# A change in who rounds tokens and who multiplies mean by rstd in a fused attention and FFN block

## The chip, the cores and the metric

The kernel runs on one core of one Trainium2 chip. The metric is the device time of one execution in microseconds; the median of several runs counts. The engines are PE (TensorE), DVE (VectorE), ACT (ScalarE), POOL (GpSimd) and SP (SyncE). Each works through its own queue in order, and they meet at semaphores.

## What is computed

One transformer block over 2048 tokens of width 128, modulated by a conditioning vector c:

```python
mod = silu(c) @ wmod              # sa, ca, ga, sb, cb, gb
h = layernorm(x) * (1 + ca) + sa
x = x + ga * (softmax(causal((h@Wq+bq) @ (h@Wk+bk).T / sqrt(128))) @ (h@Wv+bv) @ Wo + bo)
h = layernorm(x) * (1 + cb) + sb
mask = top-4 of 16 blocks of softmax(h @ w_router + b_router)
x = x + gb * (sum over blocks of mask * relu(h @ w1_block + b1_block) @ w2_block + b2)
```

All is float32. Where precision counts, the kernel splits an operand into a rounded part (hi, type fp32r) and a rest (lo), and multiplies in three passes: hi by hi, lo by hi, hi by lo.

## The kernel before

The 2048 tokens are 16 tiles of 128 and four groups of 512 (`NG = 4`, `GT = 4` tiles each). Norms 0 to 3 are the first layernorm of the four groups, norms 4 to 7 the second. The projections of queries and keys are folded into one matrix (`fold_hi`, `fold_lo`), and the value and output matrices into `back`. So the attention weights multiply the normalized tokens themselves, in the halves `z_hi` and `z_lo`.

The order of work is written out by hand: one plan per engine, a list of words such as `j0` or `e12`, a letter for the kind of step and a number for its group, tile or part (lines 43 to 68). `run` calls the steps in that order, so each engine's queue is its plan. SP has no plan: it loads the inputs in order and then stores the results as they are made (lines 402 to 409).

The steps that matter here:

- ACT (`SCALAR_PLAN`): `j0` and `j1` copy the two halves of group 0's transposed tokens to `zt_hi` (line 598). `z3` makes `fold_hi` (544), `z6` copies w1, `z11` makes `lift2` (557, 558), `q` rounds the queries to `g_hi` (606), `n` the transposed norms (602), `a` applies a norm to a group as x times rstd plus a bias (591), `e` are the exponentials of one score tile, twice, to `p_hi` and `p_full` (620, 627), or once to `p_last` (618), `c` copies the context (633), `h` rounds the hidden layer (656), `y` the output.
- DVE (`VECTOR_PLAN`): `g` makes the statistics of a norm (687, 690), `z3` `fold_lo` (880), `u` `zt_lo` of group 0 (721), `z10` copies the modulation (893, 894), `v` applies norm 1 (714), `s` are the row maxima of score chunks (744, 749, 755, 759), `n` and `q` the rests (728, 733), `b` puts the maxima into a row of `g_lo` (767, 769), `i` hides later keys (778), `m` and `c` are the router's logits and the choice (832), `f` the results (863).
- POOL (`GPSIMD_PLAN`): `p` is the power (variance + eps) to -0.5 of a norm; with it go, for norms that ACT applies (2 to 7), a negated mean (428) and its product with rstd (433), which is ACT's bias. `u` are the token halves of a group: a rounding copy to `z_hi` (444) and the rest `z_lo` (445). `l` makes `p_lo` (513), `k` `hid_lo` (519).
- PE (`TENSOR_PLAN`): `n` transposes a norm, `q` projects, `a` is a score chunk for the maxima (989), `s` the scores in three passes (1028, 1029, 1041), `w` the weighted sum (929, 930, 933), `o` the output projection (1073), `m` transposes the choice (1110), `h` and `d` the two layers of the FFN.

Results go through `res`, two buffers of 512 columns for four groups. The results of groups 2 and 3 therefore wait on DVE for the stores of groups 0 and 1 (lines 860 and 900).

Of the kernel before, what the change touches and what calls it, by code (L numbers as in the profile page):

```python
# [22 lines left out]
P = 128  # L23
GT = 4
# [16 lines left out]
FIRST_MAXES = ("a0", "a1", "a2", "a3")  # L41

TENSOR_PLAN = """
i1 i0 i3 z0 i2 z10 z1 n0 z2 z6 z3 q0 z4 z7 a0 a1 a2 a3 n1 p2 p1 p0 b0 q1 s0 s1 a4 a5 z5 s2 a6 s3 a7 n2 w0 a8 a9
w1 w2 w3 a10 a11 p4 z9 p6 z8 b1 q2 o0 n3 s4 a12 p5 a13 s5 s6 a14 s7 a15 a16 w4 s8 a17 w5 a18 s9 a19 q3 a20 s10
a21 w6 a22 s11 a23 w7 a24 w8 b2 w9 a25 w10 s12 a26 s13 a27 s14 w11 s15 a28 a29 w12 s16 o1 s17 s18 s19 a30 a31
s20 w13 s21 a32 w14 a33 s22 a34 w15 a35 s23 w16 a36 a37 w17 w18 a38 a39 n4 w19 w20 b3 w21 r0 w22 s24 s25 h0 z11
s26 w23 s27 s28 m0 s29 w24 n5 o2 s30 s31 h1 s32 r1 w25 w26 w27 h2 s33 w28 s34 w29 m1 w30 h3 n6 s35 s36 s37 r2
s38 w31 w32 w33 h4 w34 w35 w36 s39 m2 w37 w38 w39 h5 d0 o3 d1 d2 d3 h6 h7 d4 h8 d5 h9 d6 n7 d7 h10 r3 d8 h11 d9
d10 m3 y0 h12 v12 h13 v13 y1 d11 h14 v14 h15 v15 d12 d13 y2 d14 d15 t0 y3 t1  # L50
"""
SCALAR_PLAN = """
z0 z1 j0 j1 z3 z6 z11 q0 z4 n1 z9 a2 q1 e0 z5 e1 e2 n2 e3 c0 z13 z12 a3 z8 q2 e4 n3 e5 e6 e7 e8 q3 e9 e10 e11
e12 e13 c1 e14 e15 e16 z7 e17 e18 e19 e20 a4 e21 n4 e22 e23 a5 e24 e25 e26 c2 m0 e27 e28 e29 n5 e30 h0 e31 e32
a6 h1 e33 m1 e34 n6 e35 e36 e37 z14 h2 h3 e38 e39 c3 h4 m2 h5 y0 h6 h7 a7 h8 n7 h9 y1 h10 m3 h11 h12 h13 y2 h14
h15 y3 z15
"""
VECTOR_PLAN = """
j0 z0 j1 a0 z1 a1 g1 z3 u0 u1 z10 g2 v1 s0 s1 s2 s3 q0 n1 b0 g3 s4 s5 z5 s6 s7 q1 s8 s9 s10 s11 n2 b1 x0 s12 s13
s14 q2 s15 s16 n3 s17 i8 s18 s19 i9 s20 s21 i10 s22 s23 s24 i11 b2 s25 z6 s26 s27 q3 s28 s29 g4 x1 g5 s30 i20  # L60
s31 s32 s33 s34 s35 i21 s36 s37 i22 s38 s39 n4 i23 b3 m0 c0 h0 x2 n5 g6 h1 m1 c1 n6 i36 h2 h3 i37 m2 i38 c2 i39
h4 h5 x3 g7 h6 h7 h8 h9 n7 h10 m3 c3 h11 f0 k12 k13 f1 k14 k15 f2 f3 t0 t1
"""
GPSIMD_PLAN = """
z0 z1 z4 j0 j1 u0 p1 z7 p2 z6 z8 l0 l1 l2 p3 u1 z11 u2 l4 l5 l6 l7 l8 l9 z10 l10 l12 l13 l14 l15 l16 l17 l18 p4
l19 l20 l21 p5 l22 z9 u3 l24 l25 l26 l27 l28 l29 l30 p6 l31 k0 l32 l33 k1 l34 l35 l36 k2 l37 l38 k3 k4 k5 p7 k6
k7 k8 k9 k10 k11 z12
"""


def adaln_attention_sparse_ffn(nc, x_in, wq_in, bq_in, wk_in, bk_in, wv_in, bv_in, wo_in, bo_in,
# [61 lines left out]
    with ExitStack() as ctx:  # L133
# [22 lines left out]
        hid_full = sb("hid_full", [P, 2, GW])  # L156
        hid_hi, hid_lo = sb("hid_hi", [P, NH, GW], F32R), sb("hid_lo", [P, NH, GW], F32R)
        y_sb = sb("y_sb", [P, 2, GW])
        res = sb("res", [P, 2, GW])
        future, unseen = sb("future", [P, GW]), sb("unseen", [P, P])  # L160

        wq, wk, wv, wo = (sb(n, [P, P]) for n in ("wq", "wk", "wv", "wo"))
# [84 lines left out]
        xn_by_act, xn_by_dve = sem("xn_by_act"), sem("xn_by_dve")  # L247
        nmax_s, score_hid = sem("nmax_s"), sem("score_hid")
        dve_step, pool_step = sem("dve_step"), sem("pool_step")
        xt_mm, nt_hi_s, nt_lo_s, z_tok_s = sem("xt_mm"), sem("nt_hi_s"), sem("nt_lo_s"), sem("z_tok_s")  # L250
        q_mm, q_hi_s, q_lo_s = sem("q_mm"), sem("q_hi_s"), sem("q_lo_s")

        turn_mm, turn_out, first_max_mm, first_max = (sem(n) for n in ("turn_mm", "turn_out", "first_max_mm", "first_max"))
# [105 lines left out]
        def store_row(queue, i):  # L359
            t = GT // 2 + i  # L360
            queue.wait_ge(row_res_s, i + 1)
            queue.dma_start(out_tiles[NG - 1][:, t:t + 1, :],
                            res[:, (NG - 1) % 2, t * P:(t + 1) * P].rearrange("p (i d) -> p i d", d=D)).then_inc(stored[NG - 1], 16)

        block = ctx.enter_context(nc.Block())

        @block.sync
        def _(sp):
            def load(dst, src, done):
                sp.dma_start(dst, src).then_inc(done, 16)  # L370
# [24 lines left out]
            load_bias(BO, bo_in, bias_vo_in_s)
            load_column(B2, b2_in, b2_in_s)
            load_x(3)
            load(b1_row[:], row(b1_in), b1_in_s)
            load(wr[:], wr_in, wr_in_s)
            load(br_row[:], row(br_in), wr_in_s)  # L400

            for n in range(NG):
                g, part = n, result_part(n)
                sp.wait_ge(res_s, n + 1)
                sp.dma_start(out_tiles[g][:, part.start // P:part.stop // P, :],
                             res[:, g % 2, part].rearrange("p (i d) -> p i d", d=D)).then_inc(stored[g], 16)
            store_row(sp, 1)
            for g in range(NG):
                sp.wait_ge(stored[g], 16 if g < NG - 1 else 48)

        @block.gpsimd
        def _(pool):
# [10 lines left out]
            def power(n):  # L423
                k, g = n // NG, n % NG
                t = slice(g * GT, g * GT + GT)
                pool.wait_ge(stats, n + 1)
                if scalar_applies(n):
                    ahead(pool.tensor_scalar(neg_mean[:, k, t], mv[:, k, t, 0], -1.0, None, ALU.mult))
                step(pool.tensor_scalar(rstd[:, k, t], mv[:, k, t, 1], EPS, None, ALU.add))
                last = pool.tensor_tensor(rstd[:, k, t], rstd[:, k, t], pow_half[:], ALU.pow)  # L430
                if scalar_applies(n):
                    step(last)
                    last = pool.tensor_tensor(mean_rstd[:, k, t], neg_mean[:, k, t], rstd[:, k, t], ALU.mult)  # L433
                last.then_inc(power_s, 1)
# [90 lines left out]
        def _(act):  # L525
# [132 lines left out]
            def y_copy(n):  # L658
# [616 lines left out]
```

## Time and profile before

| what | value |
|---|---|
| median of three runs | 113.96 us (113.64 to 114.23) |
| the profiled execution, its time | 113.55 us |
| its span, first to last instruction | 111.8 us |
| granted TensorE clock over the span | 1.0 of full |
| PE busy 15.5 to 21.7 us | 6.16 of 6.20 us |
| DVE, ACT, POOL busy in it | 5.65, 4.34, 4.85 us |
| PE busy 21.7 to 25.5 us | 3.67 of 3.80 us |
| DVE, ACT, POOL busy in it | 3.66, 3.80, 3.50 us |

The profile is of one execution. Times of rows are counted from the span's start; a row of a timeline has the start, the duration, the engine, the line of the kernel, the operation, what is written and read, the shape and the count, and in brackets the idle time of the engine ahead of it with what ended it. Neighbours on one engine overlap a little: a start to start distance is what an instruction costs its queue. PEld is PE's weight load, which runs ahead of the matmul of its line.

### The profile page before, as it was taken

The page shows a single profiled execution, that of the slowest core. Times are in us where ns is not written, and L with a number is a line of the kernel's source. Part 1 is how long each engine was busy: PE and PEld are TensorE (multiplying, and loading weights), DVE is VectorE, ACT ScalarE, POOL GpSimd, SP SyncE. Part 2 cuts the span into 40 slices and gives each one's busy share as a digit, 9 for nine tenths or more (in the row PEclk, how much of TensorE's full clock was granted, in tenths as well). Part 3 has the DMA queues.
Part 4 walks back from the last instruction along what each step waited for, and adds up shares of the span by engine and source line. Part 5 has one row for each costly group of instructions (what it writes and reads, how often), then busy time and mean ns, then how long its engine had stood idle before and what let it go on. Part 6 is the DMA issues. An engine that isn't in the chain of part 4 may idle for free.

```text
span 111.8 us, 2013 instructions
## 1 busy us (share of the span) xinstructions
PE 107.3 (96%) x585; PEld 87.3 (78%) x585; DVE 87.3 (78%) x322; ACT 74.4 (67%) x163; POOL 88.1 (79%) x119
## 2 busy tenths in 40 slices
PE   5989999999999999999999999999999999999991
PEld 2468759878888888888888787878889888877790
DVE  5999999999999999978899379915975863874451
ACT  1337298597964299778488995998833668817710
POOL 6869877998999379999999999999995688947000
DMA  2994000000000000000000000000000000003324
GB/s 53 275 339 136 3 0 6 0 3 0 0 0 3 0 6 0 0 0 3 0 0 6 0 0 0 0 0 0 0 0 6 3 3 0 0 0 94 90 69 128
DMA packets 5879, 3.42 MB, mean 31 GB/s; under 512 B 743, under 2 KB 5483, under 8 KB 5868
## 3 DMA queue, kind: packets, MB, share of 16 engines
q1 hardware_dynamic: 5292, 3.03, 9.2%
q10 hardware_dynamic: 576, 0.26, 0.8%
q8 instruction: 5, 0.08, 0.3%
q14 instruction: 6, 0.05, 0.2%
HBM read 2.24 MB, written 1.05 MB: 29 GB/s over the span
## 4 chain that ended last, share of the span: by engine, by line
PE 81%; DVE 13%; issue 2%; POOL 2%
PE bank L929 14%; PE bank L930 13%; PE bank L933 13%; PE bank L1041 8%; PE bank L989 7%; PE bank L1029 6%; PE bank L1028 6%; PE bank L1073 3%; PE bank L963 2%; PE bank L1139 2%; DVE nmax L744 1%; DVE st L687 1%; PE bank L1168 1%; POOL rstd L440 1%; DVE xn L714 1%
## 5 line engine op out<-in xcount | busy, mean ns | idle before, releaser
L513 POOL TENSOR_TENSOR p_lo<-p_full,p_hi 128x512 fp32r<-128x512 f32 (+2 forms) x36 | 42.5, 1202 | 4.5 <-ACT p_full L627 4.5
L620 ACT ACTIVATE p_hi<-bank 128x512 fp32r<-128x512 f32 (+2 forms) x36 | 20.6, 571 | 6.5 <-PE bank L933 2.9
L627 ACT ACTIVATE p_full<-bank 128x512 f32<-128x512 f32 (+2 forms) x36 | 20.5, 569 | 0.6 <-POOL p_lo L513 0.6
L519 POOL TENSOR_TENSOR hid_lo<-hid_full,hid_hi 128x512 fp32r<-128x512 f32 x12 | 15.5, 1296 | 5.2 <-ACT hid_hi L656 5.2
L749 DVE TENSOR_REDUCE cmax<-bank 128x1 f32<-128x512 f32 x24 | 16.1, 685 | 1.9 <-PE bank L989 1.7
L1028 PE MATMUL bank<-g_hi,zt_hi 128*128 128x512 f32 (+3 forms) x40 | 15.2, 380 | 0.0
L1041 PE MATMUL bank<-g_lo,zt_hi 128*128 128x512 f32 (+3 forms) x40 | 14.6, 373 | 0.2 <-DVE g_lo L769 0.2
L1029 PE MATMUL bank<-g_hi,zt_lo 128*128 128x512 f32 (+3 forms) x40 | 14.5, 364 | 0.0
L929 PE MATMUL bank<-p_hi,z_hi 128*128 128x512 f32 (+2 forms) x36 | 14.0, 389 | 0.0
L989 PE MATMUL bank<-zt_hi,g_hi 128*128 128x512 f32 (+3 forms) x40 | 13.8, 386 | 0.0
L930 PE MATMUL bank<-p_hi,z_lo 128*128 128x512 f32 (+2 forms) x36 | 13.4, 373 | 0.0
L933 PE MATMUL bank<-p_lo,z_hi 128*128 128x512 f32 (+2 forms) x36 | 13.4, 373 | 0.0
L842 DVE SCALAR_TENSOR_TENSOR hid_full<-bank,keep 128x512 f32<-128x512 f32 x12 | 8.1, 686 | 5.6 <-POOL hid_lo L519 2.7
L591 ACT ACTIVATE xn<-x,mean_rstd,rstd 128x127 f32<-128x127 f32 x24 | 9.9, 484 | 0.3 <-POOL mean_rstd L433 0.3
L656 ACT CAST hid_hi<-hid_full 128x512 fp32r<-128x512 f32 x12 | 7.4, 623 | 3.0 <-DVE hid_full L842 2.4
L1041 PEld LDWEIGHTS bank<-g_lo,zt_hi 128*128 128x128 f32 x40 | 7.5, 188 | 1.7 <-issue 0.7
L989 PEld LDWEIGHTS bank<-zt_hi,g_hi 128*128 128x128 f32 x40 | 7.5, 189 | 1.4 <-ACT g_hi L606 0.2
L1028 PEld LDWEIGHTS bank<-g_hi,zt_hi 128*128 128x128 f32 x40 | 7.5, 189 | 1.1
L1029 PEld LDWEIGHTS bank<-g_hi,zt_lo 128*128 128x128 f32 x40 | 7.6, 189 | 0.9
L430 POOL TENSOR_TENSOR rstd<-rstd,pow_half 128x4 f32<-128x4 f32 x7 | 7.3, 1038 | 0.6
L929 PEld LDWEIGHTS bank<-p_hi,z_hi 128*128 128x128 f32 x36 | 6.8, 188 | 1.2
L933 PEld LDWEIGHTS bank<-p_lo,z_hi 128*128 128x128 f32 x36 | 6.8, 188 | 1.2
(213 smaller groups left out, 256.0 us busy)
## 6 DMA issues: line engine op xcount, KB each, us to landing
x<-in_L_attn_y_all_dram SPq DMA_DIRECT2D x3, 256.0 KB, 3.3
out_dram<-res SPq DMA_DIRECT2D x3, 256.0 KB, 2.3
w<-in_L_ffn_w_dram SPq DMA_DIRECT2D x2, 256.0 KB, 3.9
x<-in_L_attn_y_all_dram SPq DMA_DIRECT2D x2, 128.0 KB, 2.9
wmod<-in_L_wmod_dram SPq DMA_DIRECT2D x1, 256.0 KB, 3.6
wmod<-in_L_wmod_dram ACTq DMA_DIRECT2D x1, 128.0 KB, 3.2
out_dram<-res SPq DMA_DIRECT2D x1, 128.0 KB, 1.9
wk<-in_L_attn_Wk_dram SPq DMA_DIRECT2D x1, 64.0 KB, 2.9
```

Source lines behind the costliest of these rows:

```text
L513: pool.tensor_tensor(p_lo[:, s, w:], p_full[:, n % 2, w:], p_hi[:, s, w:].bitcast(F32), ALU.subtract).then_inc(p_lo_pool, 1)
L519: pool.tensor_tensor(hid_lo[:, m, :], hid_full[:, n % 2, :], hid_hi[:, m, :].bitcast(F32), ALU.subtract).then_inc(hid_lo_pool, 1)
L620: nc.scalar.activation(p_hi[:, s, w:], src, ACT.Exp).then_inc(p_hi_s, 1)
L627: nc.scalar.activation(p_full[:, n % 2, w:], src, ACT.Exp).then_inc(p_full_s, 1)
L749: nc.vector.tensor_reduce(cmax[:, n, c:c + 1], src, AX.X, ALU.max, negate=True).then_inc(turn_out, 1)
L929: mm(dst, w_hi, m_hi, start=start, stop=False)
L930: mm(dst, w_lo, m_hi, start=False, stop=False)
L933: return mm(dst, w_hi, m_lo, start=False, stop=stop)
L989: last = mm(dst[:, 0:w], tile(g_hi, g * GT + r), zt_hi[:, c * GW:c * GW + w], start=True, stop=not masked)
L1028: mm(dst[:, w:], tile(zt_hi, j), high, start=True, stop=False)
L1029: mm(dst[:, w:], tile(zt_lo, j), high, start=False, stop=False)
L1041: last = mm(dst[:, w:], tile(zt_hi, j), g_lo[:, g * GW + w:(g + 1) * GW], start=False, stop=not diag)
```

## The change

Three things, and no word of any plan changes its place among the others:

1. The rounding copy to `z_hi` goes from POOL to ACT (`token_high`, plan words `u0` to `u3`). `u0` stands between `j0` and `j1`, `u1` and `u2` between `e3` and `c0`, `u3` between `q2` and `e4`. POOL waits for it by a new semaphore, `z_hi_s`, ahead of `z_lo`.
2. For norms 4 to 7 POOL makes the power alone, and DVE makes minus mean times rstd in one instruction (`shift_mean`, words `e4` to `e7`). They stand between `s33` and `s34`, `n4` and `i23`, `m1` and `c1`, `h7` and `h8`. ACT's apply waits for `shifted_mean`. Norms 2 and 3 stay as they were.
3. `res` has four buffers in place of two, and the waits for stores in `finish` and `row_finish` are gone.

```diff
-        res = sb("res", [P, 2, GW])
+        res = sb("res", [P, NG, GW])
...
                 pool.wait_ge(stats, n + 1)
-                if scalar_applies(n):
+                if scalar_applies(n) and n < NG:
                     ahead(pool.tensor_scalar(neg_mean[:, k, t], mv[:, k, t, 0], -1.0, None, ALU.mult))
                 step(pool.tensor_scalar(rstd[:, k, t], mv[:, k, t, 1], EPS, None, ALU.add))
                 last = pool.tensor_tensor(rstd[:, k, t], rstd[:, k, t], pow_half[:], ALU.pow)
-                if scalar_applies(n):
+                if scalar_applies(n) and n < NG:
                     step(last)
                     last = pool.tensor_tensor(mean_rstd[:, k, t], neg_mean[:, k, t], rstd[:, k, t], ALU.mult)
...
             def token_halves(g):
-                pool.wait_ge(*norm_applied(g))
-                step(pool.tensor_copy(tokens(z_hi, g), norm_rows(g)))
+                pool.wait_ge(z_hi_s, g + 1)
                 pool.tensor_tensor(tokens(z_lo, g), norm_rows(g), tokens(z_hi, g).bitcast(F32),
...
             def apply(n):
                 k = n // NG
-                act.wait_ge(power_s, n + 1)
+                if n < NG:
+                    act.wait_ge(power_s, n + 1)
+                else:
+                    act.wait_ge(shifted_mean, n - NG + 1)
...
+            def token_high(g):
+                act.wait_ge(*norm_applied(g))
+                nc.scalar.copy(tokens(z_hi, g), norm_rows(g)).then_inc(z_hi_s, 1)
...
+            def shift_mean(n):
+                k, g = n // NG, n % NG
+                t = slice(g * GT, g * GT + GT)
+                dve.wait_ge(power_s, n + 1)
+                nc.vector.scalar_tensor_tensor(out=mean_rstd[:, k, t], in0=mv[:, k, t, 0], scalar=-1.0, in1=rstd[:, k, t],
+                                               op0=ALU.mult, op1=ALU.mult).then_inc(shifted_mean, 1)
...
             def finish(n):
                 g, part = n, result_part(n)
-                if g >= 2:
-                    dve.wait_ge(stored[g - 2], 16)
                 dve.wait_ge(y_turned, n + 1)
-                nc.vector.tensor_tensor(res[:, g % 2, part], result_bank(n)[:, part],
+                nc.vector.tensor_tensor(res[:, g, part], result_bank(n)[:, part],
...
                 if i == 0:
                     dve.wait_ge(x_due_s, 1)
-                    dve.wait_ge(stored[NG - 3], 16)
```

## Rows read from the trace of the kernel before

**Rows 1.** Page, part 1: busy us (share of span) x instructions, by engine.

```profile
PE 107.3 (96%) x585; PEld 87.3 (78%) x585; DVE 87.3 (78%) x322; ACT 74.4 (67%) x163; POOL 88.1 (79%) x119
```

**Rows 2.** Busy time by stretch: PE, PEld, DVE, ACT, POOL.

```profile
25.50:109.00 83.50, 83.50 (x447) 69.44 (x446) 63.72 (x226) 59.14 (x125) 67.76 (x69) 1.00 0.03 9
```

**Rows 3.** Chain that ended last, in order of time: start us, us, what.

```profile
8.25 0.38 DVE mv L690 x4
8.65 0.29 DVE fold_lo L880
```

**Rows 4.** Timelines of PE and DVE around the first finished scores.

```profile
15.53 0.47 PE L1041 MATMUL bank<-g_lo,zt_hi 128*128 128x512 f32 x1 [0.19 <-DVE g_lo L769]
16.14 0.23 PE L1043 MATMUL bank<-ident_b,causal 128*128 128x128 bf16 x1
16.38 0.53 PE L989 MATMUL bank<-zt_hi,g_hi 128*128 128x512 f32 x2
16.89 0.69 DVE L749 TENSOR_REDUCE cmax<-bank 128x1 f32<-128x512 f32 x1 [0.31 <-PE bank L989]
```

**Rows 5.** Timeline of PE's weight loads, output projection of group 0.

```profile
24.89 0.52 PEld L1073 LDWEIGHTS bank<-back,ctx_sb 128*128 128x128 f32 x4 [0.32 <-DVE g_lo L767]
```

**Rows 6.** Groups by shape (busy us, mean ns), then ACT's timeline.

```profile
L444 POOL CAST z_hi<-xn 128x512 fp32r<-128x512 f32 x4 | 2.4, 612 | 0.7 <-DVE xn L707 0.7
L656 ACT CAST hid_hi<-hid_full 128x512 fp32r<-128x512 f32 x12 | 7.4, 623 | 3.0 <-DVE hid_full L842 2.4 <-PE bank L933 0.5
...
86.64 0.62 ACT L656 CAST hid_hi<-hid_full 128x512 fp32r<-128x512 f32 x1 [0.87 <-DVE hid_full L842]
87.16 0.58 ACT L644 COPY keep<-bank 128x512 bf16<-128x512 bf16 x1
```

**Rows 7.** Timeline of ACT, rows behind the places of the casts 1 to 3.

```profile
21.34 0.59 ACT L633 COPY ctx_sb<-bank 128x512 f32<-128x512 f32 x1 [1.40 <-PE bank L1059]
...
26.31 0.60 ACT L620 ACTIVATE p_hi<-bank 128x512 fp32r<-128x512 f32 x1 [0.69 <-PE bank L1041]
```

**Rows 8.** Timelines of ACT and of PE's weight loads, 7.7 to 15.7 us.

```profile
7.72 0.65 ACT L598 CAST zt_hi<-bank 128x256 fp32r<-128x256 f32 x2
8.34 0.28 ACT L544 ACTIVATE fold_hi<-bank 128x128 fp32r<-128x128 f32 x1
...
10.13 0.17 ACT L558 COPY lift<-mod 128x1 f32<-128x1 f32 x1
10.37 0.59 ACT L606 CAST g_hi<-bank 128x512 fp32r<-128x512 f32 x1
...
15.67 0.57 ACT L606 CAST g_hi<-bank 128x512 fp32r<-128x512 f32 x1
...
11.05 0.19 PEld L989 LDWEIGHTS bank<-zt_hi,g_hi 128*128 128x128 f32 x1 [0.24 <-ACT g_hi L606]
```

**Rows 9.** Timelines of POOL and DVE around norm 4's power.

```profile
50.44 0.20 POOL L433 TENSOR_TENSOR mean_rstd<-neg_mean,rstd 128x4 f32<-128x4 f32 x1
...
50.93 0.57 DVE L755 CUSTOM_DVE_ANT_0 bank<-bank,future 128x384 f32<-128x384 f32 x1 [0.16 <-PE bank L989]
...
51.59 0.16 DVE L759 TENSOR_REDUCE nmax<-cmax 128x1 f32<-128x4 f32 x1
51.66 0.29 DVE L778 TENSOR_TENSOR bank<-bank,unseen 128x128 f32<-128x128 f32 x1
```

**Rows 10.** Timelines of DVE and of PE's weight loads at the first choice.

```profile
61.03 0.69 DVE L832 TENSOR_TENSOR chosen<-marked,bank 128x512 bf16<-128x512 f32 x1
61.90 0.23 PEld L1110 LDWEIGHTS bank<-ident_b,chosen 128*128 128x128 bf16 x4 [0.27 <-DVE chosen L832]
```

**Rows 11.** Timeline of DVE, the third result.

```profile
106.80 0.69 DVE L863 TENSOR_TENSOR res<-bank,x 128x512 f32<-128x512 f32 x1
```

**Rows 12.** Timeline of DVE, two zt_lo of 128x512.

```profile
14.12 0.68 DVE L728 TENSOR_TENSOR zt_lo<-bank,zt_hi 128x512 fp32r<-128x512 f32 x1
...
23.04 0.68 DVE L728 TENSOR_TENSOR zt_lo<-bank,zt_hi 128x512 fp32r<-128x512 f32 x1
```

More of the change, by code:

```diff
@@ L43 @@
 TENSOR_PLAN = """
[L44 to L48, printed above, removed]
@@ L49 @@
-s38 w31 w32 w33 h4 w34 w35 w36 s39 m2 w37 w38 w39 h5 d0 o3 d1 d2 d3 h6 h7 d4 h8 d5 h9 d6 n7 d7 h10 r3 d8 h11 d9
-d10 m3 y0 h12 v12 h13 v13 y1 d11 h14 v14 h15 v15 d12 d13 y2 d14 d15 t0 y3 t1
+i1 i0 i3 z0 i2 z10 z1 n0 z2 z6 z3 q0 z4 z7 a0 a1 a2 a3 n1 p2 p1 p0 b0 q1 s0 s1 a4 a5 z5 s2 a6 s3 a7 n2 w0 a8
+a9 w1 w2 w3 a10 a11 p4 z9 p6 z8 b1 q2 o0 n3 s4 a12 p5 a13 s5 s6 a14 s7 a15 a16 w4 s8 a17 w5 a18 s9 a19 q3 a20
+s10 a21 w6 a22 s11 a23 w7 a24 w8 b2 w9 a25 w10 s12 a26 s13 a27 s14 w11 s15 a28 a29 w12 s16 o1 s17 s18 s19 a30
@@ L51 @@
+a31 s20 w13 s21 a32 w14 a33 s22 a34 w15 a35 s23 w16 a36 a37 w17 w18 a38 a39 n4 w19 w20 b3 w21 r0 w22 s24 s25
+h0 z11 s26 w23 s27 s28 m0 s29 w24 n5 o2 s30 s31 h1 s32 r1 w25 w26 w27 h2 s33 w28 s34 w29 m1 w30 h3 n6 s35 s36
+s37 r2 s38 w31 w32 w33 h4 w34 w35 w36 s39 m2 w37 w38 w39 h5 d0 o3 d1 d2 d3 h6 h7 d4 h8 d5 h9 d6 n7 d7 h10 r3
+d8 h11 d9 d10 m3 y0 h12 v12 h13 v13 y1 d11 h14 v14 h15 v15 d12 d13 y2 d14 d15 t0 y3 t1
 """
 SCALAR_PLAN = """
-z0 z1 j0 j1 z3 z6 z11 q0 z4 n1 z9 a2 q1 e0 z5 e1 e2 n2 e3 c0 z13 z12 a3 z8 q2 e4 n3 e5 e6 e7 e8 q3 e9 e10 e11
@@ L54 @@
-e12 e13 c1 e14 e15 e16 z7 e17 e18 e19 e20 a4 e21 n4 e22 e23 a5 e24 e25 e26 c2 m0 e27 e28 e29 n5 e30 h0 e31 e32
-a6 h1 e33 m1 e34 n6 e35 e36 e37 z14 h2 h3 e38 e39 c3 h4 m2 h5 y0 h6 h7 a7 h8 n7 h9 y1 h10 m3 h11 h12 h13 y2 h14
-h15 y3 z15
+z0 z1 j0 u0 j1 z3 z6 z11 q0 z4 n1 z9 a2 q1 e0 z5 e1 e2 n2 e3 u1 u2 c0 z13 z12 a3 z8 q2 u3 e4 n3 e5 e6 e7 e8 q3
+e9 e10 e11 e12 e13 c1 e14 e15 e16 z7 e17 e18 e19 e20 a4 e21 n4 e22 e23 a5 e24 e25 e26 c2 m0 e27 e28 e29 n5 e30
+h0 e31 e32 a6 h1 e33 m1 e34 n6 e35 e36 e37 z14 h2 h3 e38 e39 c3 h4 m2 h5 y0 h6 h7 a7 h8 n7 h9 y1 h10 m3 h11
@@ L57 @@
+h12 h13 y2 h14 h15 y3 z15
 """
 VECTOR_PLAN = """
[L59 to L62, printed above, removed]
+j0 z0 j1 a0 z1 a1 g1 z3 u0 u1 z10 g2 v1 s0 s1 s2 s3 q0 n1 b0 g3 s4 s5 z5 s6 s7 q1 s8 s9 s10 s11 n2 b1 x0 s12
@@ L63 @@
+s13 s14 q2 s15 s16 n3 s17 i8 s18 s19 i9 s20 s21 i10 s22 s23 s24 i11 b2 s25 z6 s26 s27 q3 s28 s29 g4 x1 g5 s30
+i20 s31 s32 s33 e4 s34 s35 i21 s36 s37 i22 s38 s39 n4 e5 i23 b3 m0 c0 h0 x2 n5 g6 h1 m1 e6 c1 n6 i36 h2 h3 i37
+m2 i38 c2 i39 h4 h5 x3 g7 h6 h7 e7 h8 h9 n7 h10 m3 c3 h11 f0 k12 k13 f1 k14 k15 f2 f3 t0 t1
 """
 GPSIMD_PLAN = """
-z0 z1 z4 j0 j1 u0 p1 z7 p2 z6 z8 l0 l1 l2 p3 u1 z11 u2 l4 l5 l6 l7 l8 l9 z10 l10 l12 l13 l14 l15 l16 l17 l18 p4
-l19 l20 l21 p5 l22 z9 u3 l24 l25 l26 l27 l28 l29 l30 p6 l31 k0 l32 l33 k1 l34 l35 l36 k2 l37 l38 k3 k4 k5 p7 k6
@@ L67 @@
-k7 k8 k9 k10 k11 z12
+z0 z1 z4 j0 j1 u0 p1 z7 p2 z6 z8 l0 l1 l2 p3 u1 z11 u2 l4 l5 l6 l7 l8 l9 z10 l10 l12 l13 l14 l15 l16 l17 l18
+p4 l19 l20 l21 p5 l22 z9 u3 l24 l25 l26 l27 l28 l29 l30 p6 l31 k0 l32 l33 k1 l34 l35 l36 k2 l37 l38 k3 k4 k5
+p7 k6 k7 k8 k9 k10 k11 z12
 """
@@ L249, in adaln_attention_sparse_ffn @@
         dve_step, pool_step = sem("dve_step"), sem("pool_step")
-        xt_mm, nt_hi_s, nt_lo_s, z_tok_s = sem("xt_mm"), sem("nt_hi_s"), sem("nt_lo_s"), sem("z_tok_s")
+        xt_mm, nt_hi_s, nt_lo_s, z_hi_s, z_tok_s, shifted_mean = (
+            sem(n) for n in ("xt_mm", "nt_hi_s", "nt_lo_s", "z_hi_s", "z_tok_s", "shifted_mean"))
         q_mm, q_hi_s, q_lo_s = sem("q_mm"), sem("q_hi_s"), sem("q_lo_s")
@@ L362, in store_row @@
             queue.dma_start(out_tiles[NG - 1][:, t:t + 1, :],
-                            res[:, (NG - 1) % 2, t * P:(t + 1) * P].rearrange("p (i d) -> p i d", d=D)).then_inc(stored[NG - 1], 16)
+                            res[:, NG - 1, t * P:(t + 1) * P].rearrange("p (i d) -> p i d", d=D)).then_inc(stored[NG - 1], 16)
         block = ctx.enter_context(nc.Block())
@@ L405, in _ @@
                 sp.dma_start(out_tiles[g][:, part.start // P:part.stop // P, :],
-                             res[:, g % 2, part].rearrange("p (i d) -> p i d", d=D)).then_inc(stored[g], 16)
+                             res[:, g, part].rearrange("p (i d) -> p i d", d=D)).then_inc(stored[g], 16)
             store_row(sp, 1)
@@ L665, in y_copy @@
                 nc.scalar.activation(y_sb[:, g % 2, part], y_bank(n)[:, part], ACT.Identity, bias=gbb2[:]).then_inc(y_out, 1)
-            run(SCALAR_PLAN, {"z": prepare, "j": first_high, "a": apply, "n": norm_high, "q": q_high, "e": exps, "c": ctx_copy,
+            run(SCALAR_PLAN, {"z": prepare, "j": first_high, "a": apply, "n": norm_high, "q": q_high, "u": token_high, "e": exps, "c": ctx_copy,
                               "m": keep_copy, "h": hidden, "y": y_copy})
@@ L899, in row_finish @@
                     dve.wait_ge(x_due_s, 1)
-                    dve.wait_ge(stored[NG - 3], 16)
                 dve.wait_ge(row_mm, i + 1)
-                nc.vector.tensor_tensor(res[:, (NG - 1) % 2, t * P:(t + 1) * P], row_bank(i)[:, 0:P], x_due[:, i, :],
+                nc.vector.tensor_tensor(res[:, NG - 1, t * P:(t + 1) * P], row_bank(i)[:, 0:P], x_due[:, i, :],
                                         ALU.add).then_inc(row_res_s, 1)
@@ L918, in _ @@
             nc.vector.tensor_copy(ident_b[:], ident[:]).then_inc(copies_made, 1)
-            run(VECTOR_PLAN, {"z": prepare, "j": first_stat, "a": first_apply, "v": apply, "u": first_low, "g": norm_stats, "n": norm_low, "q": q_low, "s": row_max, "b": shift,
+            run(VECTOR_PLAN, {"z": prepare, "j": first_stat, "a": first_apply, "v": apply, "u": first_low, "g": norm_stats, "e": shift_mean, "n": norm_low, "q": q_low, "s": row_max, "b": shift,
                               "i": hide, "l": split, "x": attention_out, "m": logits, "c": choose, "h": hidden, "k": hidden_low, "f": finish, "t": row_finish})
```

## The prediction

> **What bounds the kernel now.** I read the busy shares first: PE is busy for 107.3 of 111.8 us [rows 1]. A share is a mean over stages, so I cut the span next: from 25.5 to 109.0 PE is busy for all 83.50 us, while POOL works 67.76, DVE 63.72 and ACT 59.14 of them [rows 2]. In that stretch no engine but PE can hand time back, and anything that holds PE adds to the end one for one. Before it the picture is different. The chain of waits, in order of time, runs over DVE from the second group's aggregates at 8.25 through fold_lo at 8.65 [rows 3], on through zt_lo and the maxima of group 0, up to the first finished score matmul, which PE starts at 15.53 after waiting for DVE's g_lo [rows 4]. Then PE and DVE share the chain until 24.89, where PE resumes the output projection of group 0 after DVE's last g_lo copy [rows 5]. From there on it is PE to the end. So there are two questions: what the change does to the DVE and ACT steps before 24.9, and whether it ever makes PE wait after that.
>
> **The change, part by part.**
>
> Token rounding, taken off POOL. Four casts go, 612 ns each, 2.4 us in all [rows 6]. POOL is off the chain in the full stretch, so this gives PE nothing. On ACT each costs what its sister does, the SBUF to SBUF cast hid_hi of the same size: 623 ns alone, and 0.52 us of ACT's queue, since the copy behind the one at 86.64 starts at 87.16 [rows 6].
>
> Two of the new casts, for groups 1 and 2, stand between p_last of group 0 and the context copy at 21.34, which waited 1.40 us for PE [rows 7]: 2 x 0.52 = 1.04 us fits, with 0.36 us over. The third, for group 3, stands behind g_hi of group 2 and ahead of the exponential at 26.31, which waited 0.69 us for PE [rows 7]: 0.52 fits, with 0.17 over. Were that cover gone, an ACT delay would show in the score banks and then in PE, one for one; the price would be the 0.2 to 0.5 us by which the casts stick out.
>
> The cast for group 0 has no cover. It is put between the two halves of the first zt_hi copy, ahead of fold_hi. In the trace those two halves take 0.65 us from 7.72 and fold_hi starts at 8.34, with no idle time marked before it [rows 8]. The token cast's input is ready (DVE has written xn at 7.44), so it runs at once, from about 8.0, and fold_hi moves by the queue cost, less at most 0.05 of slack: from 8.34 to about 8.83, ending at 9.11 instead of 8.62. On DVE the aggregates are through at 8.63 and fold_lo starts at 8.65 [rows 3], so DVE has no slack either: fold_lo, zt_lo, the copy of the modulation, group 2's statistics, xn of group 1 and the four maxima all move by 0.49. That is why the cost reaches the end: everything in DVE's queue is held by one instruction that waits for ACT.
>
> How much of it survives. On the ACT and PE side lift2 waits for DVE and moves by 0.49, so its second part starts at 10.62 instead of 10.13. g_hi of group 0 started at 10.37, held by PE and not by ACT; now ACT is free for it about 0.1 behind 10.62, at 10.72: 0.35 later [rows 8]. PE's first max matmul, whose weights waited for g_hi at 11.05, follows by 0.32 to 0.35 [rows 8]. PE is then back to back up to the transposes of group 1, and ACT back to back behind them to g_hi of group 1 at 15.67 [rows 8], which moves by 0.33. DVE's line brings the first score from 15.53 to 16.02. But PE then stood from the mask matmul at 16.14 to 16.38, where such a matmul takes 0.05 elsewhere, so 0.19 of waiting for g_hi of group 1 (15.67 + 0.57 = 16.24) is in that row [rows 4]. It absorbs 0.19 of the 0.49: both sides meet at 16.38 + 0.30 to 0.33. DVE's next maximum, at 16.89, had waited 0.31 for exactly this matmul [rows 4], so DVE's own 0.49 gives 16.58 + 0.49 = 17.07, below 16.89 + 0.31 = 17.20. From there to 24.89 both engines are chained without a gap that could take more: PE waited for DVE at 24.89 [rows 5]. Term: +0.31 us.
>
> Bounds for that term: above, the whole 0.52 of the cast if the gap at 16.14 closes for another reason; below, 0.0 if fold_hi were held by something other than ACT's queue. A gain is excluded for the term itself, since work is only added ahead of a step on the chain. I take 0.31, the value at which both sides meet.
>
> Waits of POOL. z_lo now waits for ACT's cast instead of following POOL's own. For group 0 it starts at about 8.65 instead of 8.20, and behind it in POOL's queue stand the norm powers of groups 1 and 2. Group 1's power ended at 10.80 and would end at 11.25; DVE comes to its xn of group 1 at 10.90 before and at 11.39 after, so it still does not wait. For groups 1 to 3 ACT is ahead of POOL and the wait costs nothing.
>
> Mean times rstd of norms 4 to 7. Per norm POOL loses a negation of about 0.24 us with the gap behind it and the product of 0.20 us at 50.44 with the wait ahead of it [rows 9]; together some 0.55 us, four times, about 2 us. DVE gets one 128x4 operation each time. No such operation of DVE with a scalar and two SBUF inputs is in the trace; the nearest row is the 128x4 reduction at 51.59, 0.16 us alone and 0.07 of the queue, since the next starts at 51.66 [rows 9]. I take 0.08 to 0.15 of queue, bounded by 0.0 and 0.3. For norm 4 it is queued between two row maxima, right when POOL's power ends (about 50.1), and delays the next maximum by about 0.1; the one after that waited 0.16 for PE at 50.93 [rows 9], so nothing goes further. For norm 5 it stands ahead of the last mask and the g_lo copies, and DVE then runs without a gap to the choice at 61.03, which ends at 61.72; PE's weight load for it started at 61.90 [rows 10]. DVE needs about 0.1 to reach PE, which leaves 0.08: a delay of 0.07 to 0.15 may put 0 to 0.07 on PE. I take 0.02. Norm 6's operation sits ahead of a choice with about half a microsecond to spare, and norm 7's where DVE waited for POOL anyway. Term: +0.02, range 0 to 0.2.
>
> Four result buffers. Two waits of DVE on stores are dropped. The third result at 106.80 waited for no store (no idle time is shown before it; the row before it on DVE ends at 106.76) [rows 11], and the first store had landed long before. 0.0, both ways.
>
> A rule to weigh against the first term. The trace says that the move is no gain in itself: 612 ns on POOL against 623 on ACT [rows 6]. What POOL's part could do is slow DVE beside it. The Trainium skill, GPSIMD Engine Reference, section Key points, says that GpSimd and VectorE share their SBUF interfaces and contend when VectorE runs in a two-port mode or has two SBUF inputs. By it, DVE would speed up once POOL's casts are gone, and the sum would be rival 4's instead of the one below; the rows there do not bear it out.
>
> **Sum.** The profiled execution took 113.55 us for a span of 111.8; 113.55 + 0.31 + 0.02 = 113.88. The median of the runs is 113.96, 0.41 above the profiled one, so for the median: 113.96 + 0.33 = 114.29, say 114.3. A measurement of this kernel tells about 0.5% (0.57 us) from no change, so this counts as no change.
>
> **Rivals.**
> 1. Everything passes, nothing is absorbed: the gap at 16.14 doesn't take its 0.19, because g_hi of group 1 moves by 0.49 too, and the full queue time of the cast, 0.52, arrives at 24.89, with 0.07 at the choice: 113.96 + 0.59 = 114.55. For it: ACT is back to back there. Against it: g_hi of group 0 had been waiting for PE.
> 2. Slower for good, by one mechanism in the middle: norm 4's new operation blocks DVE's queue, row maxima behind it, until POOL's power is done. POOL is the busiest engine after PE there [rows 2]. Up to about 1 us of lateness PE's turn banks cover it; if POOL's power came 1.5 us later than DVE gets there, PE would stand 0.5 us: 113.96 + 0.33 + 0.5 = 114.8. Against it: the seven p_lo ahead of the power run back to back, so its place is fixed, and by the rows it ends as DVE arrives.
> 3. Absorbed: fold_hi was held by PE's product at 8.31 and not by ACT, and DVE finds room behind it: 114.0.
> 4. Faster by the freed POOL: it writes and reads less beside DVE, and DVE's chain before 24.89 gets shorter. Two casts lie there or just before it; if DVE ran at half pace beside each 0.61 us of them, 0.3 us apiece would come back: 113.96 + 0.33 - 0.6 = 113.7. Against it: DVE's zt_lo of 128x512 took 0.68 us at 14.12 beside tiny POOL work, and at 23.04, behind the cast and beside z_lo, 0.68 again [rows 12]. For a gain over 0.57 us even that is not enough.
>
> **How the numbers follow.** Forecast (0.15 to 0.45 slower): 0.56. Rival 1: 0.14. Rival 2: 0.10. Rival 3: 0.12. Rival 4 and other gains: 0.08. The range takes the forecast, rivals 1 and 3, and part of 2; with 0.2 us on each side for a median of three runs that lay between 113.64 and 114.23, it is 113.8 to 114.8. Slower by over 0.5% needs 114.53: rival 2 whole, half of rival 1, and little of the forecast: 0.21. Faster by over 0.5% needs 113.39: 0.04. Within: 0.75.
>
> **What would show it.** Right: fold_hi starts near 8.8 and fold_lo near 9.1; the first finished score near 16.0; the maximum of 16.89 near 17.2; PE resumes the projection at 25.2 instead of 24.89 and is full from there on, with every later row 0.3 later; POOL's share falls by about 4 us; the row of the context copy still waits for PE. Wrong: a new idle time of PE behind 25.5, a g_hi cast on the chain, the first choice reached later by DVE than by PE's weight load, or matmuls of 128x512 spaced otherwise than the 0.23 us of before. The last would outweigh all of this: 0.003 us on each of some 300 such matmuls is 0.9 us, and no row here says what sets it.

## The result: 1.0 us slower

The changed kernel took 114.93 us in the median of four runs (114.88 to 114.96); the kernel before, beside it, 113.91. The ratio is 1.0088, with an interval of 1.0061 to 1.0115. The forecast was 114.3 us, counted as no change, and its range ended at 114.8.

The head of the page of the kernel after, busy us and share of the span, then the chain that ended last (compare [rows 1]):

```profile
span 113.1 us, 2007 instructions
PE 108.4 (96%) x585; PEld 87.0 (77%) x585; DVE 89.1 (79%) x326; ACT 75.9 (67%) x167; POOL 84.0 (74%) x107
...
PE 78%; DVE 14%; issue 3%; ACT 2%; POOL 1%
```

POOL went from 88.1 to 84.0 us, as expected, and DVE from 87.3 to 89.1, which four instructions of 0.15 us do not explain. DVE's part in the chain grew from 13% to 14%, and ACT is now in it.

Where the time came in is seen when each matmul of one trace is held against the same matmul of the other. These are rows of PE's timeline after, at the places where the distance changes (start, duration, line; the lines of after are 11 higher for PE):

```profile
25.71 0.60 PE L974 MATMUL bank<-ident,xn 128*128 128x128 f32 x4
...
52.12 1.03 PE L1000 MATMUL bank<-zt_hi,g_hi 128*128 128x512 f32 x2
52.98 0.39 PE L940 MATMUL bank<-p_hi,z_hi 128*128 128x512 f32 x1
...
58.88 0.47 PE L1052 MATMUL bank<-g_lo,zt_hi 128*128 128x512 f32 x1
59.19 0.40 PE L1039 MATMUL bank<-g_hi,zt_hi 128*128 128x512 f32 x1
...
76.62 0.63 PE L974 MATMUL bank<-ident,xn 128*128 128x128 f32 x4
```

Before, they started at 25.44, 51.75, 52.20, 57.76, 57.99 and 75.30: later by 0.27, 0.37, 0.78, 1.12, 1.20 and 1.32 us. Between these places the distance stands still, to 0.04. So there is one delay before 25 us, of 0.27, and three later ones: 0.51 at 52 us (0.78 less 0.27), 0.42 at 58 (1.20 less 0.78), 0.12 by 76 (1.32 less 1.20). The last matmuls are 1.35 later in these two traces; the medians of the runs are 1.02 apart, since the profiled execution before was 0.36 below its median (113.55 against 113.91).

The first delay is the one forecast. ACT and DVE after, beside [rows 8] and [rows 3]:

```profile
7.97 0.62 ACT L613 CAST z_hi<-xn 128x512 fp32r<-128x512 f32 x1
8.49 0.37 ACT L601 CAST zt_hi<-bank 128x256 fp32r<-128x256 f32 x1
8.75 0.29 ACT L544 ACTIVATE fold_hi<-bank 128x128 fp32r<-128x128 f32 x1
...
9.07 0.29 DVE L892 SCALAR_TENSOR_TENSOR fold_lo<-bank,fold_hi 128x128 fp32r<-128x128 f32 x1 [0.45 <-ACT fold_hi L544]
...
15.98 0.47 PE L1052 MATMUL bank<-g_lo,zt_hi 128*128 128x512 f32 x1 [0.19 <-DVE g_lo L783]
16.66 0.53 PE L1000 MATMUL bank<-zt_hi,g_hi 128*128 128x512 f32 x2
```

The cast of group 0 takes 0.52 us of ACT's queue (7.97 to 8.49), fold_hi goes from 8.34 to 8.75, fold_lo from 8.65 to 9.07 and now waits 0.45 for ACT. The first finished score is 0.45 later than in [rows 4], the maximum chunk behind it 0.28: the gap ahead of it took the rest.

The three later delays stand in DVE's timeline after, at the new instruction of norms 4, 5, 6 and 7, with what POOL did at the time:

```profile
49.73 0.69 DVE L763 TENSOR_REDUCE cmax<-bank 128x1 f32<-128x512 f32 x1 [0.23 <-PE bank L1000]
50.34 1.12 DVE L729 SCALAR_TENSOR_TENSOR mean_rstd<-mv,rstd 128x4 f32<-128x4 f32 x1
51.38 0.68 DVE L763 TENSOR_REDUCE cmax<-bank 128x1 f32<-128x512 f32 x1
...
56.86 0.58 DVE L729 SCALAR_TENSOR_TENSOR mean_rstd<-mv,rstd 128x4 f32<-128x4 f32 x1
...
72.27 0.57 DVE L729 SCALAR_TENSOR_TENSOR mean_rstd<-mv,rstd 128x4 f32<-128x4 f32 x1
...
92.95 0.15 DVE L729 SCALAR_TENSOR_TENSOR mean_rstd<-mv,rstd 128x4 f32<-128x4 f32 x1
```

```profile
49.15 1.04 POOL L431 TENSOR_TENSOR rstd<-rstd,pow_half 128x4 f32<-128x4 f32 x1
50.16 2.53 POOL L513 TENSOR_TENSOR p_lo<-p_full,p_hi 128x512 fp32r<-128x512 f32 x2
...
56.69 0.74 POOL L513 TENSOR_TENSOR p_lo<-p_full,p_hi 128x256 fp32r<-128x256 f32 x1 [0.39 <-ACT p_full L634]
...
71.54 1.29 POOL L513 TENSOR_TENSOR p_lo<-p_full,p_hi 128x512 fp32r<-128x512 f32 x1
...
91.86 1.04 POOL L431 TENSOR_TENSOR rstd<-rstd,pow_half 128x4 f32<-128x4 f32 x1
93.06 1.30 POOL L519 TENSOR_TENSOR hid_lo<-hid_full,hid_hi 128x512 fp32r<-128x512 f32 x1 [0.17 <-ACT hid_hi L663]
```

One instruction of 128x4 takes 1.12, 0.58, 0.57 and 0.15 us. The rows speak against a wait for its semaphore: POOL's power of norm 4 ended at 50.19, when DVE was still inside the row maximum of 49.73, and the product began at 50.34, right behind that maximum. Each of the long ones begins while POOL is inside p_lo, and ends within 0.02 us of that p_lo: 56.86 + 0.58 = 57.44 against 56.69 + 0.74 = 57.43, and 72.27 + 0.57 = 72.84 against 71.54 + 1.29 = 72.83. At norm 4 it ends at 51.46, and the first of POOL's two p_lo of 1.29 us began at 50.16, so it ended at 51.45. At norm 7 the product begins at 92.95, between the end of the power at 92.90 and the start of POOL's next instruction at 93.06, and takes 0.15.

What that costs shows in PE's weight loads. The maxima behind the held instruction empty the two banks that the next chunks need:

```profile
52.12 0.19 PEld L1000 LDWEIGHTS bank<-zt_hi,g_hi 128*128 128x128 f32 x1 [0.38 <-DVE cmax L763]
52.65 0.19 PEld L1000 LDWEIGHTS bank<-zt_hi,g_hi 128*128 128x128 f32 x1 [0.34 <-DVE cmax L769]
```

### The profile page after: what moved, and what is told of

Read it like the earlier page. It is cut to its first block, busy times and chain, and to the rows that moved or that the text cites. A ratio compares the mean times of both kernels' runs of the same rounds, so it can differ in the third digit from the quotient of the medians.

```text
span 113.1 us, 2007 instructions
## 1 busy us (share of the span) xinstructions
PE 108.4 (96%) x585; PEld 87.0 (77%) x585; DVE 89.1 (79%) x326; ACT 75.9 (67%) x167; POOL 84.0 (74%) x107
## 3 DMA queue, kind: packets, MB, share of 16 engines
HBM read 2.24 MB, written 1.05 MB: 29 GB/s over the span
## 4 chain that ended last, share of the span: by engine, by line
PE 78%; DVE 14%; issue 3%; ACT 2%; POOL 1%
PE bank L940 13%; PE bank L941 12%; PE bank L944 12%; PE bank L1052 8%; PE bank L1000 7%; PE bank L1040 6%; PE bank L1039 6%; PE bank L1084 3%; PE bank L974 2%; DVE g_lo L781 2%; PE bank L1150 2%; DVE nmax L758 1%; PE bank L1179 1%; DVE bank L769 1%; PE bank L1144 1%
```

## The experiments

The theory from here on: a DVE instruction with two tensor inputs in SBUF (the memory of the kernel's `sb` tiles, which the matmul banks are not part of), which begins while POOL is inside an instruction that reads SBUF, is held until that one ends. The first rival is that POOL's power comes too late for DVE; the second that the casts of ACT, or z_lo's new wait, are behind the middle delays too. The first four kernels ran beside runs of the kernel before with a median of 113.71 us, the last four beside ones with 113.61; "above before" is meant against these. What was expected in absolute times was reckoned from the 113.91 of the result.

**One input in place of two.** The same product by four instructions, each with one tensor input and rstd as a scalar per partition:

```diff
-                nc.vector.scalar_tensor_tensor(out=mean_rstd[:, k, t], in0=mv[:, k, t, 0], scalar=-1.0, in1=rstd[:, k, t],
-                                               op0=ALU.mult, op1=ALU.mult).then_inc(shifted_mean, 1)
+                for i in range(g * GT, g * GT + GT):
+                    last = nc.vector.tensor_scalar(mean_rstd[:, k, i:i + 1], mv[:, k, i, 0:1], rstd[:, k, i:i + 1], -1.0,
+                                                   ALU.mult, ALU.mult)
+                last.then_inc(shifted_mean, 1)
```

> The changed kernel, but mean times rstd is made by four DVE tensor_scalar instructions of 128x1 per norm: one SBUF tensor input, with rstd as the per-partition scalar, in place of one instruction of 128x4 with two SBUF tensor inputs. Theory (two-input lock: a DVE instruction with two SBUF inputs that starts while POOL is inside an instruction that reads SBUF is held until that one ends): no instruction of this line is longer than about 0.2 us, the four together cost DVE's queue 0.3 us, PE's delays of 0.51 at 52 us, 0.42 at 58 us and 0.12 at 76 us shrink to 0.2 in all or less; 114.1 to 114.3 us, that is 0.7 below the changed kernel. Rival (POOL's power comes too late, DVE waits for the semaphore): nothing changes, or it gets 0.2 worse with four instructions; 114.9 to 115.1 us. Rival (any read of rstd by DVE beside POOL is held): each of the four, or the first, is as long as 0.5 to 1.1 us; 114.9 us or more.

Measured: 114.36 us, 0.65 above before, ratio 1.0059 (1.0044 to 1.0074). DVE's groups by shape (busy us, mean ns), of after and of this kernel, then this kernel's timeline at norm 4:

```profile
L729 DVE SCALAR_TENSOR_TENSOR mean_rstd<-mv,rstd 128x4 f32<-128x4 f32 x4 | 2.4, 609 | 0.0
```

```profile
L730 DVE TENSOR_SCALAR mean_rstd<-mv,rstd 128x1 f32<-128x1 f32 x16 | 2.3, 205 | 0.0
```

```profile
50.40 0.57 DVE L730 TENSOR_SCALAR mean_rstd<-mv,rstd 128x1 f32<-128x1 f32 x4
50.88 0.68 DVE L765 TENSOR_REDUCE cmax<-bank 128x1 f32<-128x512 f32 x1
...
50.19 2.54 POOL L513 TENSOR_TENSOR p_lo<-p_full,p_hi 128x512 fp32r<-128x512 f32 x2
```

None of the sixteen is held, though POOL is inside p_lo from 50.19: they take 203 to 208 ns. PE's delay at 52 us is gone. What stays is 0.3 before 25 us, 0.4 at norm 5 and 0.1 at norm 6, since four instructions cost DVE's queue 0.48 us (50.40 to 50.88), more than the 0.3 expected. By this the time was a miss: 0.2 to 0.4 above before was expected, and it is 0.65. The interval also touches that of the changed kernel (from 1.0061), so it is the lengths in the trace, and not the time, that speak against both rivals of this run.

This run changes the operation and the shape along with the number of inputs. The changed kernel itself has a closer comparison: hid_full is the same operation on 128x512, with one input in a bank and one in SBUF. Its twelve instructions (ns, shortest/median/longest), and one of them inside a POOL instruction:

```profile
L856 DVE SCALAR_TENSOR_TENSOR hid_full<-bank,keep x12: 661/692/693, 64.2 to 100.6; 128x512 f32<-128x512 f32 x12
```

```profile
85.36 0.68 DVE L856 SCALAR_TENSOR_TENSOR hid_full<-bank,keep 128x512 f32<-128x512 f32 x1
...
85.32 1.29 POOL L519 TENSOR_TENSOR hid_lo<-hid_full,hid_hi 128x512 fp32r<-128x512 f32 x1
```

It is not held, though it began 0.04 us after POOL's.

**Two inputs, with POOL kept out.** The changed kernel, and POOL waits behind each power of norms 4 to 7 until the product is made:

```diff
                 last.then_inc(power_s, 1)
+                if n >= NG:
+                    pool.wait_ge(shifted_mean, n - NG + 1)
```

> The changed kernel, but POOL, behind each power of norms 4 to 7, waits for DVE's product before it goes on to its next instruction, so that POOL reads nothing while DVE's two-input instruction runs. Theory (two-input lock): DVE's instruction takes 0.15 us at all four norms, as at norm 7 in the changed kernel; POOL loses 0.2 to 0.4 us four times, which it has; PE's three delays go but for 0.1; 114.1 to 114.3 us. Rival (late power): DVE's instruction and PE's delays stay as they are, and POOL is later: 114.9 us or more.

Measured: 113.93 us, 0.22 above before, ratio 1.0023 (1.0011 to 1.0035).

DVE's group by shape, then the timeline at norm 4:

```profile
L731 DVE SCALAR_TENSOR_TENSOR mean_rstd<-mv,rstd 128x4 f32<-128x4 f32 x4 | 0.6, 154 | 0.0
```

```profile
50.46 0.15 DVE L731 SCALAR_TENSOR_TENSOR mean_rstd<-mv,rstd 128x4 f32<-128x4 f32 x1
50.53 0.69 DVE L765 TENSOR_REDUCE cmax<-bank 128x1 f32<-128x512 f32 x1
...
49.28 1.04 POOL L431 TENSOR_TENSOR rstd<-rstd,pow_half 128x4 f32<-128x4 f32 x1
50.69 2.54 POOL L515 TENSOR_TENSOR p_lo<-p_full,p_hi 128x512 fp32r<-128x512 f32 x2 [0.36 <-DVE mean_rstd L731]
```

The instruction is the same, and takes 154 ns at all four norms and 0.07 us of the queue. All three middle delays are gone; the matmuls from 26 us to the end are 0.37 to 0.40 later than in the trace before. That is 0.1 more ahead of 25 us than in the trace of the changed kernel (0.27), and what adds it is open. A wait was added to the kernel, and it became 0.74 us faster by its ratio (1.0088 less 1.0023, of 113.9; the intervals are apart). A power that came too late could not be mended in this way. The time is 0.2 above the kernel before, at the lower end of what the theory gave.

**The casts alone**, with the buffers, and POOL making the product as before (`e4` to `e7` out of DVE's plan, `power` and ACT's `apply` as before).

> The casts on ACT and the four result buffers alone; POOL makes the negated mean and the product for norms 4 to 7, as before. Theory: only the delay ahead of fold_hi is left, 0.27 us of PE at 25 us and nothing after; 114.1 to 114.3 us. Rival (ACT's casts or the z_lo waits are behind the middle delays too): PE is still held at 52 or 58 us; 114.6 us or more.

Measured: 113.88 us, 0.17 above before, ratio 1.0024 (1.0010 to 1.0037), 0.27 us by it; expected were 0.2 to 0.4. In the timelines of DVE and PE fold_lo is late. DVE's rows around 50 us have the spacing of the kernel before: the 128x384 instruction starts 0.83 later than in [rows 9], as late as PE's rows are in this trace, and waits 0.16 for PE as there:

```profile
9.09 0.29 DVE L889 SCALAR_TENSOR_TENSOR fold_lo<-bank,fold_hi 128x128 fp32r<-128x128 f32 x1 [0.47 <-ACT fold_hi L544]
...
50.31 1.29 DVE L760 TENSOR_REDUCE cmax<-bank 128x1 f32<-128x512 f32 x2 [0.23 <-PE bank L997]
51.76 0.57 DVE L766 CUSTOM_DVE_ANT_0 bank<-bank,future 128x384 f32<-128x384 f32 x1 [0.16 <-PE bank L997]
...
8.93 0.66 PE L1225 MATMUL bank<-ident,w 128*128 128x128 f32 x4 [0.63 <-DMA w<-in_L_ffn_w_dram]
```

In this one execution w1's load landed late and held PE by 0.8 us at 8.93, so the trace doesn't size the early delay, but it shows that nothing is added after 25.44, where PE is 0.85 late, up to the end, where it is 0.85.

**The product alone**, with the buffers, and the casts back on POOL (`u0` to `u3` out of ACT's plan).

> The product on DVE and the four result buffers alone; POOL rounds the tokens as before. Theory (two-input lock): no delay before 25 us, and the delays of 0.5, 0.4 and 0.1 at norms 4 to 6 are back: 0.7 to 1.05 above before, 114.6 to 115.0 us; DVE's instruction is held at norms 4, 5 and 6 until the POOL instruction that started behind the power ends, wherever that now lies. Rival (the delays need the casts' shift): close to before, 113.9 to 114.1 us.

Measured: 115.00 us, 1.29 above before, ratio 1.0110 (1.0085 to 1.0135). The product takes 1.13, 0.59, 0.57 and 0.15 us, and PE's delay grows from 0.18 at 26 us to 1.22 at 75, as after (0.27 to 1.32). The timelines of DVE and POOL at norm 4:

```profile
50.25 1.13 DVE L730 SCALAR_TENSOR_TENSOR mean_rstd<-mv,rstd 128x4 f32<-128x4 f32 x1
...
50.07 2.53 POOL L514 TENSOR_TENSOR p_lo<-p_full,p_hi 128x512 fp32r<-128x512 f32 x2
```

So the product alone brings back the middle delays, 1.04 us of PE in this trace. In size the time is a miss: 0.7 to 1.05 above before was expected, and it is 1.29, with an interval from 0.97. No delay was expected ahead of 25 us either, and there are 0.18; 0.14 of them begin at 8.28, where PE's weight load waited 0.18 us for w1's load, which has nothing to do with the product. Whether this kernel differs from the whole change is not resolved: the intervals overlap.

**The cast of group 0 under cover.** From the kernel in which POOL waits, with `u0` behind `z6` in ACT's plan and, on POOL, behind the power of norm 1:

```diff
-z0 z1 j0 u0 j1 z3 z6 z11 q0
+z0 z1 j0 j1 z3 z6 u0 z11 q0
...
-z0 z1 z4 j0 j1 u0 p1 z7 p2
+z0 z1 z4 j0 j1 p1 u0 z7 p2
```

> The kernel in which POOL waits for the product (which had 113.93 us, 0.22 above before), and the cast of group 0 moved on ACT from between the halves of zt_hi to behind fold_hi and the copy of w1, where ACT waited 0.46 us for DVE; on POOL z_lo of group 0 goes behind the power of norm 1. Theory (the cast of group 0 delays fold_hi): fold_lo starts at 8.65 again, PE's delay at 25 us falls from 0.3 to 0.1 or less; 113.7 to 113.9 us, as before or up to 0.2 below the kernel it is made from. Rival (what is left of the excess comes from the other casts or from noise): fold_lo is early and PE at 25 us is still 0.3 late.

Measured: 113.69 us against 113.61 before, ratio 1.0005 (0.9986 to 1.0024). The timelines of ACT and DVE:

```profile
8.32 0.28 ACT L546 ACTIVATE fold_hi<-bank 128x128 fp32r<-128x128 f32 x1
8.76 0.58 ACT L555 COPY w_t<-bank 128x512 f32<-128x512 f32 x1 [0.16 <-PE bank L1230]
9.24 0.62 ACT L615 CAST z_hi<-xn 128x512 fp32r<-128x512 f32 x1
9.81 0.40 ACT L559 ACTIVATE lift<-base,one_cb 128x127 f32<-128x127 f32 x1
...
8.63 0.29 DVE L894 SCALAR_TENSOR_TENSOR fold_lo<-bank,fold_hi 128x128 fp32r<-128x128 f32 x1
```

The cast runs at 9.24, where ACT had waited for DVE; lift2 starts at 9.81, as before (9.83); fold_lo is back at 8.63. PE is level with the trace before from 16.4 us on, to 0.05.

**The cast of group 0 back on POOL**, groups 1 to 3 on ACT, POOL waiting for the product.

> The kernel in which POOL waits for the product, with the cast of group 0 given back to POOL; groups 1 to 3 stay on ACT. Theory: nothing of the delay before 25 us is left, and the other casts, which lie under ACT's waits, cost nothing; same as before to 0.1 us, 113.7 to 113.8 us. Rival: the casts of groups 1 to 3 or DVE's 0.07 to 0.1 us per product reach PE; 113.9 us or more.

Measured: 113.63 us, ratio 1.0005 (0.9987 to 1.0023). PE is 0.03 late at 16.4 and 0.11 at the end. So the other casts and DVE's product, when it is not held, cost 0.1 us or nothing.

**The buffers alone.**

> The kernel before with four result buffers and without the two waits for stores, nothing else. Theory: no difference, 113.7 us, ratio 1.000 within 0.2%. Rival (the waits held the last results, or the longer buffer costs): 0.3 us or more either way.

Measured: 113.58 us, ratio 0.9998 (0.9981 to 1.0015). No difference.

**The suspected cost doubled.** In the changed kernel DVE makes the product twice, the first time into a tile that nobody reads:

```diff
+                nc.vector.scalar_tensor_tensor(out=neg_mean[:, k, t], in0=mv[:, k, t, 0], scalar=-1.0, in1=rstd[:, k, t],
+                                               op0=ALU.mult, op1=ALU.mult)
                 nc.vector.scalar_tensor_tensor(out=mean_rstd[:, k, t], in0=mv[:, k, t, 0], scalar=-1.0, in1=rstd[:, k, t],
```

> The changed kernel with the suspected cost doubled: DVE makes the product of norms 4 to 7 twice in a row, first into a tile that nobody reads, then into the real one, both with two SBUF inputs. Theory, first form (the pair goes over only at an instruction's end, and DVE, once it has it, keeps it for what is queued): the first is held as before (1.12, 0.58, 0.57 us) and the second takes 0.15; 0.1 to 0.3 above the changed kernel, 115.0 to 115.2 us. Second form (POOL's next instruction gets in between): the second is held for one more POOL instruction of 1.3 us at norms 4 and 6, and 1.3 at norm 5; PE loses up to 1.3 more each time, 116 to 118 us. Rival (the operation is slow in itself or by its distance to the power, 0.6 to 1.1 us each): both are equally long.

Measured: 115.23 us, ratio 1.0144 (1.0131 to 1.0157). Against the changed kernel that is 0.30 more in the medians and in the two traces (the last matmuls are 1.65 and 1.35 later than before), as the first form had it (0.1 to 0.3), but 0.6 more by the ratios, whose runs of the kernel before differ by 0.3; the time alone doesn't size it. The lengths do fit the first form; timelines of DVE and POOL at norm 4:

```profile
50.40 1.11 DVE L729 SCALAR_TENSOR_TENSOR neg_mean<-mv,rstd 128x4 f32<-128x4 f32 x1
51.44 0.15 DVE L731 SCALAR_TENSOR_TENSOR mean_rstd<-mv,rstd 128x4 f32<-128x4 f32 x1
...
50.21 2.54 POOL L513 TENSOR_TENSOR p_lo<-p_full,p_hi 128x512 fp32r<-128x512 f32 x2
```

The first is held and takes 1.11 us, the second gets through in 0.15, although POOL's two p_lo run on without a gap. By the trace POOL's second p_lo starts at 51.45, 0.02 us behind the second product, so DVE is the first of the two this time. So what is paid is the rest of the one POOL instruction that DVE meets, once. The second costs DVE's queue 0.07 (51.44 to 51.51).

## Why the prediction was wrong

- *PE has no room after 25.5 us, and any hold reaches the end.* Right: each delay stands unchanged from its place to the end.
- *The cast of group 0 delays fold_hi, and 0.19 of it is absorbed: +0.31.* Right in place and in way. fold_hi moved by 0.41 and not 0.49: it had more slack than the 0.05 allowed. Before, it started 0.03 us ahead of the half copy's end (8.34 against 8.37); after, 0.11 ahead (8.75 against 8.49 + 0.37), as neighbours on ACT do. PE moved by 0.27 at 25 us. With the casts alone it is 0.17 us in the medians and 0.27 by the ratio. Moving the cast away took it back.
- *The other casts cost nothing, POOL is freed of 4 us, and the buffers change nothing.* Right: ratio 1.0005 with groups 1 to 3 on ACT, 0.9998 for the buffers, and POOL's 88.1 less 84.0 us. The context copy still waits 0.38 us for PE, and 0.36 was forecast.
- *DVE's product takes 0.08 to 0.15 us of queue, bounded by 0.0 and 0.3, and puts +0.02 us on PE.* This is the step that failed. The nearest row was taken from a reduction with one input [rows 9], and the prediction itself said that no row had a scalar and two SBUF inputs. Free of POOL the price is right, 0.15 alone and 0.07 of the queue. Held, it took 1.04, 0.51 and 0.50 us of the queue at norms 4, 5 and 6 (50.34 to 51.38, 56.86 to 57.37, 72.27 to 72.77), and PE lost 0.51, 0.42 and 0.12. A bound from what the operation can meet was at hand in the trace before, 1.29 us for a p_lo; it was bounded by what the operation does.
- *What PE's cover took of it.* At norm 5 the forecast left 0.08 between DVE and PE, and 0.51 less 0.08 is 0.43, where 0.42 came through. At norm 6 about half a microsecond was to spare, and 0.38 of the 0.50 was absorbed.
- *Who meets whom.* DVE comes to the product in its own order, not when the power releases it: at each of norms 4 to 6 the product starts right behind DVE's instruction ahead of it, and the power had ended 0.15, 0.56 and 0.71 us earlier (at 50.19, 56.30 and 71.57). By then POOL was 0.18, 0.17 and 0.73 us into its p_lo. POOL is at work for 67.76 of 83.50 us there [rows 2], so a meeting is likely; where in POOL's instruction DVE falls follows from the two plans, and it sets the price.
- *Rival 2*, DVE's queue blocked at norm 4 with the maxima behind it, had the place and the price (0.5; measured 0.51) and the wrong cause: lateness of POOL's power, where it was POOL's next instruction. That its number came out is luck. It also took PE's cover as 1 us. The maximum behind the product started at 51.38 and not at 50.08 + 0.27 = 50.35, so it was 1.03 late, and 0.51 of this came through: the cover was about 0.5. The four small instructions bear it out: their 0.48 at norm 4 put nothing on PE.
- *Rival 4 and the rule.* The Trainium skill, GPSIMD Engine Reference, Key points, was weighed for the casts that leave POOL, as a possible gain, and not for the operation that comes to DVE, which has the very form it names: two SBUF inputs. The Trainium skill, SBUF — State Buffer, section Who interferes with whom, is more exact: the shared pair of ports is an exclusive lock; a DVE instruction with two SBUF inputs contends with a POOL one that reads SBUF, one with at most one SBUF input outside the two-port modes does not. The traces agree: held to POOL's end within 0.02 us with two inputs, 203 to 208 ns with one.

The sum, with the terms as they were: 0.27 early + 0.51 + 0.42 + 0.12 = 1.32 us in the trace, against 0.31 + 0.02 = 0.33 forecast. In the medians it is 1.02, as the traced execution before was a short one.

## What to carry to other kernels

A small DVE operation is priced by what it can meet: if both inputs are SBUF tensors and POOL streams through SBUF, its upper bound is POOL's longest instruction, and everything behind it in DVE's queue pays. Work that needs a POOL result is a likely case, since POOL is in its next instruction as soon as the result is there (here p_lo at 50.16, behind a power that ended at 50.19). One input as a per-partition scalar, or a wait on POOL until the operation is done, takes the collision away; in the run with that wait it cost POOL 2.6 us of idle time over the four norms, which POOL had to spare here. Ahead of an instruction that the critical engine waits for there is no free place on any queue: the same cast cost 0.2 to 0.3 us between two copies (from 7.97) and nothing 1.3 us later (from 9.24), under a wait.

## What the runs showed of the hardware

- A DVE instruction with two SBUF inputs that began inside a POOL instruction ended 0.02 us behind it, after 1.12, 0.58 or 0.57 us in place of 0.15. A second one right behind is not held again (1.11 and 0.15 us), though POOL's next one follows without a gap; the second starts 0.02 us ahead of it.
- The same operation with one of its inputs in a bank took 661 to 693 ns for 128x512, inside POOL's instructions as outside them.
- Four 128x1 instructions of DVE with a scalar per partition cost 0.48 us of its queue, 0.12 each, where one of 128x4 costs 0.07 when it isn't held.
- Not tried: POOL instructions with one input, and the reverse case, in which POOL meets a long two-input instruction of DVE. Every POOL instruction met here reads two SBUF tensors and writes one, so no run tells whether its reading or its writing holds DVE; the theory's "reads" is not shown by them.
